# A three-layer graph network with learned edge masks: column terms of every fourth group from TensorE products over runs of sorted edges

## The reference

```python
f1 = relu(x[row] @ nb_W[l] + nb_b[l])
f2 = relu(x[col] @ self_W[l] + self_b[l])
h = relu(concatenate([f1, f2], axis=1) @ att1_W[l] + att1_b[l])
log_alpha = (h @ att2_W[l] + att2_b[l])[:, 0]
mask = clip(sigmoid(log_alpha) * (ZETA - GAMMA) + GAMMA, 0.0, 1.0)
rowsum = segment_sum(mask, row, n) + 1e-06
d_inv_sqrt = clip(rowsum ** (-0.5), 0.0, 10.0)
vals = mask * d_inv_sqrt[row] * d_inv_sqrt[col]
x = segment_sum(vals[:, None] * x[col], row, n)
out = out + x
```

## Time and profile before

| | |
|---|---|
| median of 3 runs | 12,707.6 us (12,700.9 to 12,740.1) |
| span of the profiled execution, first to last instruction | 9,111.0 us |
| its own time around the span | not given; the median exceeds the span by 3,596.6 us |
| mean granted TensorE clock | 0.623 of 2.4 GHz |
| busy: PE, DVE, ACT, POOL | 62%, 74%, 40%, 65% |
| setup; phase A; phase B with node products, of the first layer | 0 to 612; about 672 to 2,750; about 2,750 to 3,480 us |
| DMA | 1,272 MB, mean 140 GB/s |

### The profile page before, as it was taken

The page is one execution under the profiler, slowest core; times in us unless marked ns, Lnnn a source line. Parts: engine busy times, 40 slices in busy tenths (PEclk is TensorE's granted clock), DMA queues, the critical chain, the costliest instruction groups (busy, mean ns, idle before and its releaser), DMA issues.

```text
span 9111.0 us, 203370 instructions
## 1 busy us (share of the span) xinstructions
PE 5650.8 (62%) x43467; PEld 5151.5 (57%) x43630; DVE 6736.5 (74%) x29039; ACT 3666.1 (40%) x8663; POOL 5960.7 (65%) x6294
## 2 busy tenths in 40 slices
PE   3135555555558996555555557998555555555996
PEld 1135555545548885555555556887555555555886
DVE  8877777777777877777777777877777777776788
ACT  0013322322227883322322325885322322323886
POOL 0017777777775656777777776665777777776664
PEclk7565555555558996555555557998555555555998
DMA  1014444444456664444444446665444444445665
GB/s 24 0 48 135 132 130 131 132 130 130 133 128 206 213 206 130 132 131 130 132 130 131 132 130 176 210 212 156 132 130 130 133 130 131 132 130 146 213 211 161
DMA packets 1122388, 1272.27 MB, mean 140 GB/s; under 512 B 648596, under 2 KB 652724, under 8 KB 1122356
## 3 DMA queue, kind: packets, MB, share of 16 engines
q1 hardware_dynamic: 922676, 903.51, 32.1%
q0 software_dynamic: 199680, 368.45, 16.7%
HBM read 868.11 MB, written 403.23 MB: 140 GB/s over the span
## 4 chain that ended last, share of the span: by engine, by line
POOL 44%; issue 23%; PE 22%; DVE 8%; DMA 1%; ACT 1%; POOLq 0%; DVEq 0%; ACTq 0%; SPq 0%
POOL got L526 22%; PE bank L552 12%; POOL k_hot L526 11%; POOL g_hot L526 10%; PE bank L685 6%; DVE acc L946 2%; DVE acc L947 2%; PE bank L653 1%; PE bank L690 1%; PE bank L610 1%; PE bank L601 1%; PE bank L576 1%; DMA k_x<-kept_x 1%; DMA k_hot<-qx_table,index 0%; DVE acc L909 0%
## 5 line engine op out<-in xcount | busy, mean ns | idle before, releaser
L653 PE MATMUL bank<-p_all,onehot_t 128*128 x10032 | 2301.5, 424 | 1752.4 <-issue 1731.8
L653 PEld LDWEIGHTS bank<-p_all,onehot_t 128*128 128x128 f32 x10032 | 2186.8, 330 | 1803.4 <-issue 1803.4
L526 POOL DMA_INDIRECT got<-qx_table,index x2496 | 2376.4, 952 | 784.9 <-issue 780.3
L539 POOL DMA_INDIRECT got<-y_table,index x1248 | 1187.3, 951 | 798.8 <-issue 431.5
L798 ACT ACTIVATE small<-small 128x8 f32<-128x8 f32 x624 | 130.2, 209 | 3813.9 <-DVE small L1080 3813.9
L526 POOL DMA_INDIRECT k_hot<-qx_table,index x1248 | 1181.3, 947 | 393.7 <-issue 377.5
L526 POOL DMA_INDIRECT g_hot<-qx_table,index x1248 | 1185.6, 950 | 380.6 <-issue 380.6
L552 PE MATMUL bank<-mask,onehots 128*128 128x3 bf16 x4992 | 669.8, 184 | 986.1 <-DVE mask L1091 986.1
L552 PEld LDWEIGHTS bank<-mask,onehots 128*128 128x128 bf16 x4992 | 516.0, 104 | 1250.7 <-issue 1145.5
L1118 DVE SCALAR_TENSOR_TENSOR p_all<-iota_b,col_hi,bank 128x104 f32<-128x104 bf16 x3768 | 953.9, 317 | 341.5 <-PE bank L685 335.4
L1056 DVE TENSOR_SCALAR onehots<-iota_b,rows_b 128x128 bf16<-128x128 bf16 x5016 | 888.7, 280 | 48.0
(11 more groups left out here) (167 smaller groups left out, 8859.7 us busy)
## 6 DMA issues: line engine op xcount, KB each, us to landing
onehot_t<-look_hot SPq DMA_DIRECT2D x474, 256.0 KB
row_hot<-onehots SPq DMA_DIRECT2D x468, 256.0 KB, 3.6
k_x<-col_rows SPq DMA_DIRECT2D x318, 256.0 KB, 3.6
kept_x<-got SPq DMA_DIRECT2D x312, 256.0 KB
look_hot<-k_x SPq DMA_DIRECT2D x312, 256.0 KB, 2.1
hot_in<-row_hot SPq DMA_DIRECT2D x312, 256.0 KB
k_x<-kept_x SPq DMA_DIRECT2D x312, 256.0 KB
look_new<-row_hot SPq DMA_DIRECT2D x159, 256.0 KB
```

Source lines behind the costliest of these rows:

```text
L526: pool.indirect_dma_start(got[j][:, k, :], None, qx_table, bass.IndirectOffsetOnAxis(ap=index[j][:, k:k + 1], axis=0)).then_inc(a_got[j], 16)
L539: pool.indirect_dma_start(got[j][:, k, 0:HID], None, y_table, bass.IndirectOffsetOnAxis(ap=index[j][:, k:k + 1], axis=0)).then_inc(g_got[j ...
L653: last = mm(bank_p[h][:, k, :], onehot_t[h][:, k, :], p_all[:, ds(ids[k], 1), :].rearrange("p o d -> p (o d)"), start=True, stop=True)
```

## The change

In each quad the fourth group gathers nothing in phase A. Its column terms are summed in PSUM bank 7, on top of its row terms, by 72 f32 products on PE. For this:

- The sort key is now (block of rows, column, row) in place of (block, row, column), so that in a tile edges of the same column block (the high 7 bits, `hi`) stand together: a run. Each run is one product: a 128x128 one-hot (column's low 7 bits against lane) times the 64 columns of q of block hi, added to the tile's part of bank 7. Lanes outside the run's block match nothing of it.
- After the sort the groups are ranked by their number of runs, and reordered through HBM, so that those with fewest runs become the fourth of each quad. At most 72 runs (9 rounds of 8 slots) are allowed. The runs are found by nine rounds of max and match_replace, packed three to an int32 word, and their lane patterns gathered by 36 indirect DMAs and stored as `slot_lanes`.
- q is also kept in SBUF (`q_res`, in acc's place); x's transposes go to p_all, and POOL clears acc.
- Per quad SP broadcasts nine 256 KB slot patterns, DVE makes nine 128x1024 f32 one-hots (`build_slots`), PE runs `column_terms` after groups 0, 1 and before the row terms of group 3.
- hot_b is gone: four `hot` buffers serve transposes, stores and mask sums. PE's loop is over quads. block_of and spot_of are int32.
- POOL gathers for three groups of four, with three buffers.

The diff, cut:

```diff
+    ROUNDS = 9
+    SLOTS = ROUNDS * U
+    SLOT_BITS, PER_WORD = 10, 3
...
+                def load_slots(b, r, made):
+
+                    if made is not None:
+                        sp.wait_ge(x_made, l * (ROUNDS * QUADS) + (b * ROUNDS + made))
+                        sp.sem_inc(sp_go, 1)
+                    sp.dma_start(slot_in[r % 3], slot_lanes[ds(b * SLOTS + r * U, U), :].rearrange("k e -> (k e)")
+                                 .partition_broadcast(PARTS)).then_inc(x_in[r % 3], 16)
...
+            for i in range(PICKS):
+                pool.indirect_dma_start(
+                    picked_rows[i // CHUNK][:, i % CHUNK * PARTS:(i % CHUNK + 1) * PARTS], None, node_rows,
+                    bass.IndirectOffsetOnAxis(ap=pick_row[:, i:i + 1], axis=0)
+                ).then_inc(s_picked[i // CHUNK], 16)
...
-                    for j in range(4):
-
-                        pool.wait_ge(a_idx[j], l * (QUADS + (j < 3)) + (b + 1))
+                    for j in range(3):
+
+                        pool.wait_ge(a_idx[j], l * (QUADS + 1) + (b + 1))
...
+                pool.wait_ge(m_rows, l + 1)
+                pool.sem_inc(pool_go, 1)
+                pool.memset(acc[:, :, :], 0.0).then_inc(k_zero, 1)
...
+                def column_terms(b, j):
+
+                    n = l * QUADS + b
+                    if j == 0:
+                        pe.wait_ge(n_q, node_done(l, 0, NODE_STEPS - 1))
+                        pe.wait_ge(w_in, (n + 1) * 16)
+                        pe.sem_inc(pe_go, 1)
+                    pe.load(word, slot_word[0:1, j * U:(j + 1) * U])
+                    for r in range(3 * j, 3 * j + 3):
+                        pe.wait_ge(x_made, n * ROUNDS + (r + 1))
+                        for i in range(U):
+                            at, part = divmod((r - 3 * j) * U + i, PER_WORD)
+                            bits = pe.snap(word[at], min_val=0, max_val=BASE - 1) >> SLOT_BITS * part
+                            k = bits & U - 1
+                            s = nc.s_assert_within((bits >> 3) & PARTS - 1, 0, NB - 1,
+                                                   skip_runtime_bounds_check_because="a column's block is below BLOCKS")
+                            last = plus(bank[7][:, ds(k * HID, HID)], slot_hot[r % 2][:, i, :],
+                                        q_res[:, ds(s, 1), :].rearrange("p o d -> p (o d)"))
+                        last.then_inc(x_used[r % 2], 1)
...
+                with pe.Fori(0, QUADS) as b:
+                    for j in range(4):
+                        g = b * 4 + j
+                        if j == 2:
+                            column_terms(b, j)
+                            row_terms(1, g + 1)
+                        else:
+                            row_terms(1 - j % 2, g + 1, a_sum, l * GROUPS + g)
+                        turn_hot((j + 2) % 4, g + 2)
+                        if j == 0:
+
+                            pe.wait_ge(a_sum, l * GROUPS + g)
+                            clear(bank[7])
+                        if j < 2:
+                            column_terms(b, j)
...
+            for r in range(ROUNDS):
+                eight = picks[:, 0, r * U:(r + 1) * U]
+                link(v.max(eight, pair[r % 2]))
+                link(v.match_replace(pair[(r + 1) % 2], eight, pair[r % 2], 0.0))
...
+                    v.tensor_copy(q_res[:, of_step(s), :], bank[4 + j % 2][:, :].rearrange("p (b d) -> p b d", d=HID))
...
+                def build_slots(b, r):
+
+                    h = r % 2
+                    dve.wait_ge(x_in[r % 3], (l * (3 * QUADS) + (b * 3 + (r // 3 + 1))) * 16)
+                    dve.wait_ge(x_used[h], l * (slots_used(h) * QUADS) + (b * slots_used(h) + r // 2))
+                    v.tensor_scalar(slot_hot[h].rearrange("p k m -> p (k m)") if h == 0 else
+                                    slot_hot[h][:, :, :].rearrange("p k m -> p (k m)"),
+                                    slot_in[r % 3], part_f[:, :], None, ALU.is_equal).then_inc(x_made, 1)
...
+                        if j < 3:
+                            build_slots(b, 3 * j)
+                            build_slots(b, 3 * j + 1)
+                        build_hot((j + 2) % 4, g + 2, g, b + (j >= 2))
...
+                        if j < 3:
+                            build_slots(b, 3 * j + 2)
...
-                        build_hot(hot_b[1 - h], rows_b[1 - h], g + 1, g * 2 + 4,
-                                  (a_row, l * (GROUPS + 1) + (g + 1)), a_hotb,
-                                  (a_hotst[0], l * (2 * QUADS) + (b * 2 + (j + 1) // 2)) if h else (a_hotst[1], l * QUADS + (b + j // 2)))
```

More of the change, by code:

```diff
@@ L985, in _ @@
                     n += 1
-            done, free = keys[n % 2].bitcast(I32), keys[(n + 1) % 2].bitcast(I32)
-            link(v.tensor_scalar(free, done, PARTS - 1, None, ALU.bitwise_and))
-            v.tensor_copy(col_lo, free).then_inc(s_lo, 1)
+            done, moved = sorted_of.bitcast(I32), other.bitcast(I32)
+            own, real, group_key, runs, rank, first, rest, few, kk = (ranks[:, k, :] for k in range(9))
+            link(v.tensor_scalar(moved, done, HI_AT, None, ALU.logical_shift_right))
```

332 lines of the change are left out of this document (253 added, 79 removed).

## The result

The kernel after takes 17,323.6 us (median of 4 runs, 17,305.9 to 17,335.9) against 12,709.7 before (4 runs): ratio 1.363, 95% interval 1.361 to 1.365. The forecast was 15,300 us with a range to 16,600: the direction is right, the time is some 720 us above the range.

A forecast was written before the change was run, and what follows sets the result against it. POOL's gathers bound phase A before (40.1 us per quad), PE after (56.0): 156 x (56.0 - 40.1) = +2,480, setup +120, span 9,111, 3,597 outside it: 15,308, say 15,300 us. Range 12,400 to 16,600.

The forecast's parts named there:

- Outside the span: Whole run: 3,597 us of the 12,707.6 us median lie outside the 9,111 us span, taken as fixed.
- Rival 3: Phase A: the 3,597 us are slower gathers, 1.83 us each, quad 58.5 us falling to 56; 12,440 us, chance 0.12.
- Rival 4: Phase A: late index copies with three buffers keep POOL at 40 us per quad; no separate chance given.
- POOL from 40.1 to 30.1 us: Phase A: 8 of 32 gathers per quad go, by POOL alone worth 1,564 us.
- A column product: Phase A on PE: 72 new products per quad at 0.434 us each, 31.2 us; 0.5 us each as upper case.
- Loads and gaps on PE: Phase A: word loads and address unpacking mostly hidden; quad 56.0 us over 54.1 of work, upper bound 64.
- The clock: Phase A: PE stays at 1.2 GHz, granted clock 0.50, under the added products.
- rival 1: Phase A: PE's clock rises to 2.4 GHz; 12,830 us in full, chance 0.12, or 14,060 in part, 0.15.
- DVE's cover: Phase A: nine slot one-hots per quad, 6.2 to 11.0 us; DVE's 31.0 to 35.8 us stays hidden under PE.
- Setup: Once ahead of the first layer: ranking, slot extraction, 36 gathers and stores, +120 us, bounds 80 and 170.
- Phase B, DMA, q_res, acc: Broadcasts, second copy of q, POOL's zeroing of acc and reordered groups in phase B: all at no cost.

The follow-up runs named there:

- e1: The kernel before, unchanged, run and profiled again: 12,735.9 us, ratio 0.9996 to the kernel before; span 12,733.4 us.
- e5: The kernel before with one gather of eight in phase A (output not the reference's): 8,989.8 us.
- e8: The kernel before with phase A's gathers replaced by plain loads of the same size on POOL's queue (output not the reference's): 9,041.9 us.
- e10: The kernel before, POOL waiting in each phase A group until the first four gathers have landed before issuing the other four: 11,863.5 us, ratio 0.932.
- e14: The kernel before with a wait for the first four gathers of each eight to land, in phases A and B: 11,252.0 us, ratio 0.879.
- e6: The kernel after with one gather of eight in phase A, all 72 column products kept (output not the reference's): 14,950.7 us.
- e4: The kernel after with one column product per round instead of eight (column terms of every fourth group wrong): 12,844.1 us.
- e12: The kernel after with each column product's target fixed, its block of q still unpacked (output not the reference's): 15,296.7 us.
- e2: The kernel after with column products at fixed addresses, no words loaded or unpacked (column terms of every fourth group wrong): 14,509.8 us.
- e3: The kernel after with one slot per round unpacked, its target and block used by all eight products (column terms wrong): 14,712.6 us.
- e15: The kernel after with a wait for the first four gathers of each eight to land, in phases A and B: 15,350.8 us, ratio 1.200.
- e7: The kernel before with each row one-hot of 8 tiles made by one two-source DVE comparison instead of eight: 12,777.0 us, ratio 0.998.

## Why the prediction was wrong, step by step

**Outside the span.** It stands first because the base of the sum failed. The prediction took 3,597 us as fixed around the span. They are inside: 14.3 us per quad, lost while gathers run (e1, e5, e8, e10), and 466 us per layer outside phase A, of which a pause between gathers gives back 206 (e14); the cause of the other 260 is open. Carrying them over unchanged was nearly right as a number by luck, since the kernel after loses as much: 83.8 - 68.4 = 15.4 us per quad (e6) and 1,159 - 712 = 447 per layer. The warning was at hand: over a quarter of the time with no row to it.

**Rival 3** put the 3,597 us on slower gathers of 1.83 us each. It had the right culprit and the wrong mechanism: a gather still takes POOL 0.94 + 0.30 us (e1), but the others start their instructions late. Its price, a quad of 58.5 falling to PE's 56, did not follow: the change leaves the gathers in runs of sixteen and eight, PE itself now loses 15.4 us a quad to them, and e4, where PE has little to do, shows no gain from eight fewer. Rival 4 did not come about either: POOL waits for index copies, up to 29.6 us at once, but behind PE, not as the bound.

**POOL from 40.1 to 30.1 us.** The count was right (24 gathers, POOL 69.4 us busy in three quads), the worth was off: in usual executions POOL's own time was not the bound by itself but one link of a convoy.

**A column product.** This is the step that failed, in size, and it made the time miss the range. It was taken at 0.434 us like a row term, with 0.5 as upper bound; in eight rounds of nine it is 0.578, in the ninth 0.449. The error is 64 x 0.144 + 8 x 0.015 = 9.3 us per quad, 1,450 us in all, seven tenths of the miss of 2,020. The upper bound was made from the mask sums' 0.135 us per product with one computed address; the change's unpacking is six instructions per product, and six are no longer hidden, where four are (e12). The product itself costs what the prediction said (0.427 in e2, e3, e12).

**Loads and gaps on PE.** Taken at 1.9 us over 54.1. Measured with one gather of eight: 68.4 - 63.4 = 5.0 us. That is 3.1 us per quad too low, 480 us. With both terms e6's quad, 68.4 us, lies above the upper bound of 64 even without the slow stretches. What is left of the miss, some 90 us, is the 1.1 us per quad that the kernel after loses to gathers beyond the 14.3 of before, less small terms the other way.

**The clock.** Right, and against rival 1: 0.50 all through phase A, at 75% busy in the kernel after and at 90% in e6. The rule of the Trainium skill on which rival 1 rested (TensorE: Matmul & The Clock Gate, "What's actually happening": activity releases the clock) does not show for this kind of work here.

**DVE's cover.** The slot one-hot takes 753 to 761 ns (the prediction took 0.694) and stays hidden in the kernel after; the waits for them (x_made, x_used) cost nothing seen there. In e4, where PE would be fast, they are not hidden.

**Setup.** +97 us against 120 (80 to 170). The 36 gathers took 50 us (forecast 45), nine pairs of maximum and replace 23 (12 to 22).

**Phase B, DMA, q_res, acc.** Unchanged, as forecast: 1,159 against 1,178 us per layer.

**The sum, redone.** 156 x (83.84 - 54.74) + 97 - 3 x 18 = 4,580, against 17,334 - 12,733 = 4,601 of the two spans. With the profile that the prediction had and e6's quad for PE's (right product, right gaps), its own sum would have been 9,111 + 156 x (68.4 - 40.1) + 97 + 3,597 = 17,220. So the change is slower with or without the lost time: by 28 us per quad in one case and 29 in the other. e14 and e15, where some two fifths and one half of that time are won back, say the same: 11,252 against 15,351 us.

## What to carry to other kernels

When a profiled execution's span and the run's time differ by more than a few microseconds, the profile is of another kind of execution; look for the cause, or profile again, before building a sum on it. Price a product with computed addresses by the instructions that its engine must work through per product, and count them: up to four were free here beside 0.43 us of work, six set the pace. Long uninterrupted runs of indirect gathers slowed every other engine here; a wait for the first four to have landed, once in eight, gave 7% in phase A and 5% more with phase B.

## What the runs showed of the hardware that was not expected

- While POOL issues indirect gathers on end (16 in 20 us), instructions on PE and DVE that wait for nothing, or only for the step before on their own engine, start 0.7 to 4.2 us apart, and ACT's casts come late too; it begins some 5 to 11 us after the run's first gather and ends 2 to 3 us after its last. In PE's stretches the steps are near multiples of 0.7 us (e3: 1.40, 2.10, 2.80; e7: 0.71, 0.74, 1.39). Plain loads of the same bytes on the same engine's queue, which keep POOL busy for 0.53 us each, don't do this (e8: 9,042 us against 12,798).
- The shown profile of before has the same gathers without a pause and none of this (span 9,111 us). Why that execution escaped it stays open. The instruction queues moved 33 packets in e1 and 32 in that profile, so no row shows where instructions were held up; that it is their supply is inferred, from late steps on PE, DVE and ACT and from the count of instructions in PE's loop, not seen directly.
- TensorE stayed at its 1.2 GHz level (granted clock 0.50) through a stretch of 203 us, mostly f32 64-column products, at 90% busy (e6).
- Reading two addresses from registers cost a product nothing (0.427 us with them in e3, without in e2).
